# Splitting each weighing matmul of a two-layer interaction kernel into two matmuls of 32 stationary samples

## The reference

```
x0 = x; h = x
for W in (W0, W1):                      # W0: 39 x 39 x 128, W1: 39 x 128 x 128
    h = einsum('bid,bjd,ijh->bhd', x0, h, W)
    outs.append(h)
out = concatenate(outs, axis=1).sum(axis=-1)      # 512 x 256, float32
```

## Time and profile before

| | us |
|---|---|
| median of 3 runs | 243.16 |
| the profiled execution: its own time | 245.13 |
| its span, from the first to the last instruction | 243.3 |
| TensorE matmul busy in the span | 232.4 |
| TensorE weight load busy | 202.5 |
| VectorE busy | 174.7 |
| ScalarE busy | 168.5 |

### The profile page before, as it was taken

One profiled execution on the slowest core, in us unless ns is written; L12 is line 12 of the kernel. 1 busy time (PEld: TensorE's weight loads), 2 busy tenths in 40 slices (PEclk: granted clock), 3 DMA queues, 4 the chain that ended last, 5 costly groups with the idle time before them and its releaser, 6 DMA issues.

```text
span 243.3 us, 12097 instructions
## 1 busy us (share of the span) xinstructions
PE 232.4 (96%) x5580; PEld 202.5 (83%) x5580; DVE 174.7 (72%) x314; ACT 168.5 (69%) x313; POOL 0.6 (0%) x8
## 2 busy tenths in 40 slices
PE   1999999999999999999999999999999999999992
PEld 0588799988988998889888898888988889898981
DVE  1056999787685999999999799879979959200000
ACT  2489990071570688888969989888896998998000
POOL 0000000000000000000000000000000000000000
PEclk9999999999999999999999999999999999999997
DMA  4999800020120221611531432261153140210210
GB/s 125 388 392 398 345 12 3 4 59 3 55 58 3 55 19 27 210 17 25 161 82 22 127 117 21 38 213 14 30 172 64 24 132 2 25 33 3 19 26 22
DMA packets 15699, 21.56 MB, mean 89 GB/s; under 512 B 9504, under 2 KB 10272, under 8 KB 15264
## 3 DMA queue, kind: packets, MB, share of 16 engines
q1 hardware_dynamic: 15360, 20.35, 29.1%
q10 hardware_dynamic: 288, 0.43, 0.5%
HBM read 18.32 MB, written 0.52 MB: 77 GB/s over the span
## 4 chain that ended last, share of the span: by engine, by line
PE 89%; SPq 4%; DMA 3%; ACT 2%; issue 1%; DVE 0%
PE psum L572 34%; PE psum L552 22%; PE psum L601 19%; PE psum L522 11%; SPq L344 4%; PE psum L584 4%; DMA arena<-in_u_list 2%; ACT arena L496 2%; DMA arena<-arena 1%; DVE arena L402 0%; DVE arena L374 0%; ACT arena L482 0%
## 5 line engine op out<-in xcount | busy, mean ns | idle before, releaser
L496 ACT COPY arena<-psum 64x460 f32<-64x460 f32 x256 | 137.8, 538 | 42.6 <-PE psum L552 39.1
L572 PEld LDWEIGHTS psum<-arena 128*64 128x64 f32 x1680 | 92.0, 137 | 7.9 <-issue 7.7
L572 PE MATMUL psum<-arena 128*64 128x128 f32 x1680 | 97.8, 274 | 0.0
L392 DVE TENSOR_TENSOR arena<-arena 128x1600 f32<-128x1600 f32 x32 | 58.4, 1826 | 0.0
L395 DVE TENSOR_TENSOR arena<-arena 128x1520 f32<-128x1520 f32 x32 | 55.8, 1744 | 0.0
L552 PE MATMUL psum<-arena 64*32 64x230 f32 x2048 | 55.4, 356 | 0.0
L552 PEld LDWEIGHTS psum<-arena 64*32 64x32 f32 x2048 | 39.4, 106 | 10.1 <-issue 3.7
L601 PE MATMUL psum<-arena 128*32 128x128 f32 (+3 forms) x1196 | 46.6, 315 | 0.0
L601 PEld LDWEIGHTS psum<-arena 128*32 128x32 f32 x1196 | 42.5, 110 | 4.4 <-issue 1.5
L522 PE MATMUL psum<-arena 128*32 128x210 f32 x512 | 26.4, 369 | 5.7 <-DVE arena L374 5.3
L475 ACT COPY arena<-psum 64x420 f32<-64x420 f32 x48 | 26.5, 552 | 7.7 <-PE psum L522 7.0
(11 more groups left out here) (13 smaller groups left out, 12.4 us busy)
## 6 DMA issues: line engine op xcount, KB each, us to landing
arena<-in_x SPq DMA_DIRECT2D x32, 312.0 KB, 3.4
arena<-in_v_first SPq DMA_DIRECT2D x1, 1376.0 KB, 7.8
arena<-in_v_second SPq DMA_DIRECT2D x1, 1376.0 KB, 10.7
arena<-in_w SPq DMA_DIRECT2D x1, 1280.0 KB, 6.9
arena<-in_v_near SPq DMA_DIRECT2D x2, 640.0 KB, 12.2
arena<-in_w_ones SPq DMA_DIRECT2D x2, 448.0 KB, 10.0
arena<-in_w SPq DMA_DIRECT2D x2, 320.0 KB, 3.3
arena<-in_w SPq DMA_DIRECT2D x1, 640.0 KB, 4.3
```

Of the source, the lines that this page charges most:

```text
L392: mult(view(to + EXTRAS, TO, (10, 20), (1, 10)), view(main, T, (1, 20), (0, 10)), view(x, T, (1, 20), (1, 10)), ALU.mult)
L496: done = nc.scalar.copy(view(s0[n % 2] + EXTRAS * q * B + 8 * in_batch + 4 * odd, (B, SLOTS), (2, 2), (1, 2), rows=(HALF * q, HALF * q + H ...
L572: nc.tensor.matmul(bank_view(at + HID, (1, HID), rows=(HALF * side, HALF * side + HALF)), view(s0[n % 2] + j * B, (1, B)), view(c0 + (j - ...
```

## The change

Every weighing matmul of 64 stationary samples becomes two of 32 that stream the same 128 columns: the first for samples 0 to 31 into the first column strip of its side, the second for samples 32 to 63 into the strip beside it. The four strips are then taken by two items in turn. Slots and chunks are both cut so. The loop, the waits, the PSUM places, and what the other engines do stay as they are.

```diff
                 if i < SLOTS - EXTRAS:
                     j, side = EXTRAS + i, i % 2
-                    nc.tensor.matmul(bank_view(at + HID, (1, HID), rows=(HALF * side, HALF * side + HALF)),
-                                     view(s0[n % 2] + j * B, (1, B)), view(c0 + (j - EXTRAS) * HID, (1, HID)),
-                                     start=i < 2, stop=True, skip_group_check=True)
+                    for part in range(0, HALF, ROWS):
+                        first = HALF * side + part
+                        nc.tensor.matmul(bank_view(at + HID, (1, HID), rows=(first, first + ROWS)),
+                                         view(s0[n % 2] + j * B + part, (1, ROWS)), view(c0 + (j - EXTRAS) * HID, (1, HID)),
+                                         start=i < 2, stop=True, skip_group_check=True)
                     return
...
-                done = nc.tensor.matmul(
-                    bank_view(at + HID if near else at, (1, HID), rows=(HALF * side, HALF * side + HALF)),
-                    view(apart0 + (CHUNKS * (n % 2) + chunk) * B, (1, B), rows=rows), view(w, (1, HID), rows=rows),
-                    start=False, stop=True, skip_group_check=True)
+                for part in range(0, HALF, ROWS):
+                    first = HALF * side + part
+                    done = nc.tensor.matmul(
+                        bank_view(at + HID if near else at, (1, HID), rows=(first, first + ROWS)),
+                        view(apart0 + (CHUNKS * (n % 2) + chunk) * B + part, (1, ROWS), rows=rows),
+                        view(w, (1, HID), rows=rows), start=False, stop=True, skip_group_check=True)
```

## The result

The changed kernel takes 256.29 us (median of 4 runs, 254.19 to 256.71) against 243.03 us (4 runs, 242.10 to 243.43): 1.053 times the time before, with a 95% interval of 1.047 to 1.060. It is slower, where 242.7 us and a range up to 245.4 were forecast. Every ratio here compares runs of the same round (the kernel before has medians of 242.0 to 243.0 us in them) and leaves out slow runs, those over 1.5% above the fastest of their kernel.

A forecast was written before the change was run, and what follows sets the result against it. TensorE's chain of sums and weighing was taken as the bound up to 219.44 us. Savings of 0.23 + 0.11 + 0.10 + 0.04 = 0.48 us, taken from the runs' median, gave 242.7 us, range 241.9 to 245.4.

The forecast's parts named there:

- The turn of four: Weighing on TensorE: four records on four strips cost the same 109 ns as two on two, so 0 us change.
- the edges: Where the tile changes, shorter first loads: 0.23 us saved over 18 blocks, plus 0.11, 0.10 and 0.04 in chunk groups.
- the sum: Per weighing block: 26 ns saved at its start, 13 ns lost at its end, net 13 ns saved.
- 768 slots: Weighing on the chain: 18 blocks of some 42.7 slots, over which the cost per turn was counted.
- The hidden tail: The 105 slots behind the last sums end before the gather lands, so they neither gain nor lose.
- The 2.2 us: Time to spare between the last slots' end at 236.4 us and the gather's end at 238.57 us.
- What is hidden: Work said to cost nothing: slots behind the last sums, and some 14 more instruction packets beside other transfers.
- the first rival: TensorE's instructions don't come fast enough, rounds stretch: 2.0 us more at 13.9 ns, 17 us at 15.5; chance 0.16.
- the densest 5.00 us: Stretch in the trace before with some 360 instructions, one per 13.9 ns, held against the supply rival.
- that objection: A store of waiting instructions could have carried the dense 5 us, so it need not show a steady pace.
- the rival's other end: Supply limit of 15.5 ns per instruction: 0.95 us more a round, 17 us in all, 260 us; not read as limit.
- point of decision: Rounds of 528 instructions stretch if steady supply takes longer than 13.7 ns per instruction.

The follow-up runs named there:

- the runs that starve TensorE: Changed kernel, each slot matmul cut to 16 stationary samples and 64 columns: 255.04 us, 1.050; also with x loads and gathers cut to one row: 246.74 us, 1.015.
- the starved run without transfers: Changed kernel, slot matmuls cut to 16 samples and 64 columns, loads of x from the seventh unit and gathers cut to one row: 246.74 us, 1.015.
- the changed kernel without transfers: Changed kernel with loads of x from the seventh unit on cut to one partition and each gather to one row: 249.56 us, 1.030.
- the kernel before with the same cuts: Kernel before, with loads of x from the seventh unit on cut to one partition and each gather to one row: 241.34 us, 0.996.

## Why the prediction was wrong, point by point

**The turn of four and the edges** were right. The first records of a block are 297 ns long and a whole block takes 4.79 us against 4.81, that is 0.02 us less, where the sum had 0.013; a view in steps of 0.01 us tells no more. Weighing that isn't cut by a late block of instructions costs what the prediction said. (Its "768 slots" on the chain are items, 714 slots and 54 chunks, which changes none of its terms by 0.1 us.)

**The hidden tail** was right, but with less to spare than said. The 2.2 us were read from the end of a window of my choice, 236.40 us; the last slot before ended at 236.72, and TensorE then waited 1.89 us for the gather. After the change a late block stops the slots near their end, they end at 247.10 us, and 0.49 us are left (timelines of PE). Before:

```profile
224.93 11.79 PE L572 MATMUL psum<-arena 128*64 128x128 f32 x210
238.61 1.46 PE L584 MATMUL psum<-arena 125*64 125x128 f32 x18 [1.89 <-DMA arena<-arena]
```

After:

```profile
234.84 11.55 PE L574 MATMUL psum<-arena 128*32 128x128 f32 x413
246.68 0.42 PE L574 MATMUL psum<-arena 128*32 128x128 f32 x7 [0.29 <-issue]
247.59 1.42 PE L588 MATMUL psum<-arena 125*32 125x128 f32 x36 [0.49 <-DMA arena<-arena]
```

**The failed step is "What is hidden", where 14 more instruction packets were costed at nothing, together with the first rival's chance of 0.16.** That term measured 10.8 us in the rounds of the profiled execution, where the two spans differ by 9.0; edges and turns stood as forecast. I asked what the packets cost the other transfers (1.2% of the DMA engines) and not how long TensorE waits for one. The rival's pace was then read from the densest 5.00 us, some 360 instructions. That is hardly more than one block of 256: such a stretch can run from what has already come, whatever the supply, as the 8 ns per instruction between stops show. The prediction named that objection and gave it too little weight. The changed kernel got an instruction every 145.36 us / 9,600 = 15.1 ns, and the runs that starve TensorE give 15.3 with the transfers and 14.4 without. That the rival's other end, 15.5 ns over 10 us, comes near is luck: in those 10 us before, each block's packet had landed 2.2 us or more before the block was begun and TensorE never stopped, so the prediction was right not to read 15.5 as a limit. No row of the trace before gave the pace of the supply. The mechanism of the rival, its place, its point of decision (13.7 ns) and its sign held: idle time of PEld put down to issue in the slots is 16.2 us (the page's groups), against 7.7 before.

```profile
L574 PEld LDWEIGHTS psum<-arena 128*32 128x32 f32 x3360 | 91.4, 110 | 16.7 <-issue 16.2
```

The chance was wrong, and the top of the range with it.

What the profile before would have told: the earlier trace rows has 44 packets in 0.72 MB for 11,160 instructions, one packet per 254 of them. A round of 528 instructions takes two packets in 7.2 us, one per 3.5 us, and in the rounds before they came once in 5.2 us (the median of 25 distances). Nothing in that trace showed that one could come every 3.5 us again and again. It even held one late block, in the first stage, between 26.0 and 30.1 us with the DMA engines 84% busy with loads (timeline of PE):

```profile
27.75 1.95 PE L522 MATMUL psum<-arena 128*32 128x210 f32 x37
30.11 1.20 PE L522 MATMUL psum<-arena 128*32 128x210 f32 x20 [0.41 <-issue]
```

By the same count this stop ends at the 193rd instruction behind a multiple of 256, 1.56 us after a packet has landed. It is the only idle time of PE before that is put down to issue.

The Trainium skill ("Runtime: NRT & Kernel Launch", Instruction fetch mechanics) says that the sequencer fetches blocks of 256 instructions by a DMA queue of its own while it executes the block before. The stops at every 256th instruction agree. It calls the fetch mostly hidden, behind an issue floor of about 20 cycles; here it was not hidden once instructions were used up faster than one per 14.4 to 15.3 ns, and one per 8 ns was issued between the stops, so no such floor was seen. I had used the Trainium skill for the floor and passed over the blocks.

The trace of the starved run without transfers also has the parts of the 3.7 us of a block, as means over 37 blocks between 83.56 and 221.84 us: 1.30 us from the first instruction of a block to the start of the next packet, 1.00 us for the packet, 1.40 us from its landing to the first instruction of its block. With the transfers they are 1.42, 1.11 and 1.40 us. So in these runs a packet starts only when the block before its own is under way, and the three parts follow each other within the time of one block. What stays open is why the first and the last of them take so long.

## What to carry to other kernels

A split into more and smaller instructions is free only as long as the program itself arrives. Count the instructions of a round, divide by 256, and ask whether each block has some 4 us (here 3.7 without other transfers, 3.9 with them). A dense stretch of one or two blocks doesn't tell the sustained pace, and a long one that never stopped doesn't tell the limit. When a stop comes without a releaser, count instructions between stops; equal distances point to the supply.

## What the hardware showed beyond that

SyncE's issues of gathers seem to feel the instruction blocks too. In the changed kernel without transfers the last 14 of them took 12.09 us, in the kernel before with the same cuts 9.40 us (timelines of SP):

```profile
227.83 12.09 SPq L345 DMA_DIRECT2D arena<-arena  x14
```

```profile
222.88 9.40 SPq L345 DMA_DIRECT2D arena<-arena  x14
```

Most issues are 0.63 us apart; three in the first row are longer (its chain in order of time):

```profile
229.00 1.50 SPq L345
...
232.45 1.79 SPq L345
...
236.20 1.82 SPq L345
```

They fall on the starts of instruction packets at 229.0, 232.5 and 236.3 us. Over the whole execution 22 packets started while a gather was being issued, and each time that issue or the one behind it took 0.87 to 1.91 us; of the 68 other issues all but one took 0.60 us or less. In the kernel before with the same cuts it is so for all 12 such packets (0.99 to 1.52 us). The two go together, then; that the packets are the cause wasn't tried. The gather landed late there, TensorE was idle for 3.17 us, and its clock fell from full speed (2.4 GHz) to half of it (1.2 GHz), so that the last chunks took 2.51 us instead of 1.5:

```profile
239.62:242.79 3.17, 0.00 (x1) 0.00 (x0) 0.00 (x0) 0.00 (x0) 0.00 (x0) 0.88 0.12 26
242.79:245.30 2.51, 2.50 (x36) 1.58 (x36) 0.00 (x0) 0.00 (x0) 0.00 (x0) 0.50 0.00 0
```

In the kernel before with the same cuts TensorE didn't wait there, and the last chunks ran at full clock:

```profile
234.43:235.94 1.51, 1.50 (x22) 1.09 (x18) 0.00 (x0) 0.00 (x0) 0.00 (x0) 1.00 0.00 0
```

The idle time and the 1.0 us more in the chunks are 4.2 of the 4.4 us by which this execution lost more behind its last sums. The mean granted clock was 0.987 in it and 0.997 to 1.000 in the other three executions of that kernel, so their times hold little of the fallen clock.
